# A fused vision tower on one core: projections issued earlier, their read-back a step of its own, and a new order around them

## What is computed

```python
pooled = x.reshape(B, 12, 14, 16, 14, 16).sum(axis=(3, 5))
h = einsum('bcij,ce->bije', pooled, cw).reshape(B, 196, 192)
h = h + attention(layernorm(h), Wq, bq, Wk, bk, Wv, bv)       # one head of 192
xn = layernorm(h)
probs = softmax(xn @ w_router.T)                              # 4 experts
gate, idx = top_k(probs of each expert over the 196 tokens, 98)
y = layernorm(xn) * gamma1 + beta1
hh = each expert's chosen tokens, first 24/48/96/192 channels, @ w1.T + b1, scattered back and summed
x_mlp, qkv = hh[..., :768], hh[..., 768:]                     # 12 heads of 16
x_attn = softmax(q @ k.T / 4) @ v
y2 = concat(gelu(x_mlp), x_attn)
o = (each expert's chosen rows of y2) @ w2.T + b2, masked, times gate
return h + xn + o[..., :192] + o[..., 192:]
```

## Time and profile before

| | |
|---|---|
| median of 3 runs | 1826.68 us |
| profiled execution | 1830.25 us, its span 1828.5 us |
| mean granted clock of TensorE | 0.905 of full speed |
| TensorE (matmul) busy | 1542.0 us, 84% |
| VectorE busy | 1216.9 us, 67% |
| ScalarE busy | 848.5 us, 46% |
| one turn of the loop | 212.0 us |

### The profile page before, as it was taken

How to read it: one execution, slowest core, us unless ns; L and a number is a source line. 1 busy time by engine, 2 the same in 40 slices (tenths; PEclk the granted TensorE clock), 3 DMA queues, 4 the chain that set the end, 5 groups by cost and what they waited for, 6 DMA issues and landing times.

```text
span 1828.5 us, 34571 instructions
## 1 busy us (share of the span) xinstructions
PE 1542.0 (84%) x12440; PEld 1263.2 (69%) x12440; DVE 1216.9 (67%) x2822; ACT 848.5 (46%) x1935; POOL 249.3 (14%) x318
## 2 busy tenths in 40 slices
PE   1364689989898998989899898989899899989998
PEld 1232567768686777767677776868677687868786
DVE  3847668856788477775688577785677667573552
ACT  0101355545454454545454454444545456545653
POOL 2012002200112001200022001110022001110000
PEclk9656799988999889989899889998899899999999
DMA  8857464715664265615546156533656151112220
GB/s 218 232 155 211 116 167 117 176 27 140 150 162 111 72 166 128 174 48 151 143 119 167 36 155 157 144 98 87 166 143 161 41 150 42 41 25 47 51 58 15
DMA packets 99598, 218.03 MB, mean 119 GB/s; under 512 B 61371, under 2 KB 75877, under 8 KB 88678
## 3 DMA queue, kind: packets, MB, share of 16 engines
q10 hardware_dynamic: 11904, 149.33, 30.5%
q1 hardware_dynamic: 87526, 66.49, 15.9%
HBM read 186.57 MB, written 28.90 MB: 118 GB/s over the span
## 4 chain that ended last, share of the span: by engine, by line
PE 36%; DVE 28%; issue 21%; DMA 6%; ACT 4%; POOL 4%; SPq 1%; DVEq 0%; ACTq 0%; POOLq 0%
DVE psums L1245 10%; DVE peaks L1443 7%; PE bank L1040 6%; PE bank L945 4%; PE bank L1009 4%; PE bank L957 3%; POOL var L1572 3%; DMA qs<-shiftT 3%; PE bank L975 3%; PE bank L994 2%; PE bank L868 2%; PE bank L852 2%; DVE rows L1387 2%; PE bank L1018 1%; DVE qk L1432 1%
## 5 line engine op out<-in xcount | busy, mean ns | idle before, releaser
L1443 DVE TENSOR_REDUCE peaks<-bank 98x2 f32<-98x392 f32 x768 | 425.6, 563 | 184.8 <-PE bank L975 164.1
L1194 ACT ACTIVATE Pb<-bank 98x392 f32<-98x392 f32 x768 | 375.7, 497 | 296.3 <-PE bank L994 255.9
L1245 DVE TENSOR_REDUCE psums<-xt 112x2 f32<-112x512 f32 x672 | 429.3, 678 | 34.0 <-DMA xt<-in_x_dram 11.4
L975 PE MATMUL bank<-ks,qs 96*98 96x196 f16 x1536 | 269.5, 262 | 63.4 <-DMA ks<-qk_scratch 32.9
L1040 PE MATMUL bank<-w2T,hid 128*98 128x192 f32 x1536 | 303.1, 336 | 0.0
L994 PE MATMUL bank<-qs,ks 97*98 97x196 f16 x1536 | 270.7, 261 | 11.1 <-DMA qs<-shiftT 10.6
L975 PEld LDWEIGHTS bank<-ks,qs 96*98 96x98 f16 x1536 | 167.9, 128 | 149.6 <-DVE peaks L1443 53.3
L1040 PEld LDWEIGHTS bank<-w2T,hid 128*98 128x98 f32 x1536 | 241.1, 171 | 1.9
L1009 PE MATMUL bank<-Pb,vals 98*32 98x196 f32 x3072 | 183.0, 359 | 11.6 <-ACT Pb L1194 11.6
L994 PEld LDWEIGHTS bank<-qs,ks 97*98 97x98 f16 x1536 | 170.0, 132 | 21.6 <-DMA qs<-shiftT 12.2
L1432 DVE TENSOR_TENSOR qk<-bank,qk 96x392 f16<-96x392 f32 x128 | 71.8, 561 | 140.0 <-ACT qk L1181 131.6
(11 more groups left out here) (183 smaller groups left out, 1746.2 us busy)
## 6 DMA issues: line engine op xcount, KB each, us to landing
xt<-in_x_dram ACTq DMA_DIRECT2D x93, 1568.0 KB, 9.0
qk_scratch<-qk SPq DMA_DIRECT2D x64, 294.0 KB, 4.0
qs<-qk_scratch SPq DMA_DIRECT2D x192, 73.5 KB, 2.9
ks<-qk_scratch SPq DMA_DIRECT2D x192, 73.5 KB, 3.0
out_dram<-fin SPq DMA_DIRECT2D x64, 147.0 KB
xt<-in_x_dram SPq DMA_DIRECT2D x3, 1568.0 KB, 9.4
qs<-shiftT SPq DMA_DIRECT2D x128, 2.3 KB
hid<-in_L_ffn_w_dram SPq DMA_DIRECT2D x1, 1440.0 KB
```

Of the source, the lines that this page charges most:

```text
L975: mm = pe.matmul(peak_ps[s][0:HT, T * q:T * q + T], qs[0:KS, i % NSTACK, h, HT * q:HT * q + HT], ks[0:KS, i % NSTACK, h, :], start=True, s ...
L1194: act.activation(Pb[:, (H * i + h) % NP, :, :].rearrange("p a b -> p (a b)"), score_ps[s][0:HT, 0:2 * T], ACT.Exp, scale=float(DH) ** -0.5 ...
L1245: last = dve.tensor_reduce(psums[:, m % 2, t, 2 * p:2 * p + 2], v[:, 2 * p:2 * p + 2, :, :], AX.XY, ALU.add)
L1443: dve.tensor_reduce(peaks[:, h // 6, :, h % 6], peak_ps[s][0:HT, 0:2 * T].rearrange("p (q k) -> p q k", q=2), AX.X, ALU.max, negate=True). ...
```

## The change

- `project(i)` is split: SP's six reads become the step `stack(i)`, with a wait for the scores of the image that used that stack before. In `body`, `project(i + 3)` stands at head 10 of image i (before: `project(i + 2)` at head 1), `stack(i + 2)` at head 3 (head 0 for i = 0). `project(0, 2)` of a group moves from slot 1 into the opening (slot 99).
- `shift(i, 0)` moves from head 7 to 8 of the image before, `shift(i, 1)` from head 0 to head 2; in the opening the first one a slot later. `values` moves from head 10 to 11, three `residual` steps from 10 to 8.
- In the opening, `hidden` and `project` come ahead of the end of the last image (its last `mix` and what follows).
- The scaling in `spread` becomes the step `weigh`, before the rounds of `choose`. `TAKE` goes from 27 to 25, the tables `VECTOR` and `quiet` change, `chosen`, `spread`, `turn_u` and `project(1, 0)` are given later against the last round. `planes` stands 3.5 slots behind the last pooling piece instead of 2.2.

```diff
-def pooling(dg, m, at, more=True, turn=1.2):
+def pooling(dg, m, at, more=True, turn=1.2, behind=3.5):
...
-    ops += [(slot + 2.2, ("planes", dg, m)), (slot + 2.2 + turn, ("tok", dg, m))]
+    ops += [(slot + behind, ("planes", dg, m)), (slot + behind + turn, ("tok", dg, m))]
...
     ops += [(at, ("gate_scale", dg)), (at + 2, ("gate_logits", dg)), (at + 5, ("gates", dg)),
-            (at + 7, ("gate_rows", dg))]
+            (at + 7, ("gate_rows", dg)), (at + 7.5, ("weigh", dg))]
...
-    ops = [(at, ("turn_u", dg, 0)), (at + 0.5, ("turn_u", dg, 1)), (at + 1, ("project", dg, 0))]
+    ops = [(at, ("turn_u", dg, 0)), (at + 0.5, ("turn_u", dg, 1)), (at + 1, ("project", dg, 0)), (at + 1.7, ("stack", dg, 0))]
...
+        if i == 5:
+            ops.append(("gate8", dg))
+        if i == 0:
+            ops += [("project", dg, 1), ("stack", dg, 1)]
+        if i == 3:
+            ops.append(("project", dg, 2))
+        ops.append(("hidden", dg, i))
         if tail:
...
-        if i == 5:
-            ops.append(("gate8", dg))
-        if i == 0:
-            ops.append(("project", dg, 1))
-        ops.append(("hidden", dg, i))
         if i == 1:
             ops.append(("values", dg, 0))
...
-        if i == 4:
+        if i == 5:
             ops.append(("shift", dg, 0, 0))
...
-RESIDUAL = {(0, 5): 0, (0, 10): 1, (1, 5): 2, (1, 10): 3, (2, 5): 4, (2, 10): 5, (3, 11): 6, (4, 2): 7}
-TAKE = 27
-VECTOR = {"peak": 0.52, "choose": 0.95, "first_max": 0.52, "take": 0.9, "norm1_scale": 0.9, "norm1": 0.8, "shift1": 1,
+RESIDUAL = {(0, 5): 0, (0, 8): 1, (1, 5): 2, (1, 8): 3, (2, 5): 4, (2, 8): 5, (3, 11): 6, (4, 2): 7}
+TAKE = 25
+VECTOR = {"peak": 0.52, "choose": 1.05, "first_max": 0.52, "take": 0.9, "norm1_scale": 0.9, "norm1": 0.8, "shift1": 1,
...
-            fill[0] = [("shift", 0, i, 1)] + fill[0]
+            fill[2] = [("shift", 0, i, 1)] + fill[2]
...
-            fill[7] = [("shift", 0, i + 1, 0)] + fill[7]
-            fill[10] = [("values", 0, i + 1)] + fill[10]
+            fill[8] = [("shift", 0, i + 1, 0)] + fill[8]
+            fill[11] = [("values", 0, i + 1)] + fill[11]
         if i + 2 < GRP:
-            fill[1] = [("project", 0, i + 2)] + fill[1]
+            fill[3 if i else 0].append(("stack", 0, i + 2))
+        if i + 3 < GRP:
+            fill[10] = [("project", 0, i + 3)] + fill[10]
...
+    quiet = (int(at), H * GRP)
     at = rounds(plan, 1, int(at))
-    quiet = (at + 1, H * GRP)
-    for slot, op in in_slots(choosing(1, at + 0.5) + turning(1, at + 2.5)):
+    for slot, op in in_slots(choosing(1, at + 1) + turning(1, at + 4)):
...
+            def stack(at, G_, dg, i):
+
+                n_ = G_ * GRP + i
+                s = i % NSTACK
                 sp.wait_ge(qk_out, 16 * n_ + 16 + ONE)
-                s = i % NSTACK
+                if i >= NSTACK:
+                    for half in range(2):
+                        sp.wait_ge(score_full[half], 6 * (n_ - NSTACK) + 6)
                 for blk, (qp, kp) in enumerate(((0, 0), (0, 1), (1, 0))):
...
+            def weigh(at, G_, dg):
+                chain(at, dve.tensor_tensor(zs[:, :, 0:Z], z_tok[:, :, :, 0:Z].rearrange("p h i c -> p (h i) c"),
+                                            var[:, 7, :].unsqueeze(2).broadcast_to([HT, 2 * GRP, Z]), ALU.mult))
+                linked("weigh", 1)
```

More of the change, by code:

```diff
@@ L225, in prologue @@
     for m in range(GRP // PAIR):
-        for slot, op in pooling(0, m, steadily(pieces * m, 1), True, 1.2 if m == GRP // PAIR - 1 else 7):
+        for slot, op in pooling(0, m, steadily(pieces * m, 1), True, 1.2 if m == GRP // PAIR - 1 else 7, 2.2):
             if op[0] not in ("pool", "fetch") or (op[0] == "pool" and TILES * m + op[3] >= SETUP_TILES) \
@@ L272, in opening @@
     return plan
-RESIDUAL = {(0, 5): 0, (0, 10): 1, (1, 5): 2, (1, 10): 3, (2, 5): 4, (2, 10): 5, (3, 11): 6, (4, 2): 7}
-TAKE = 27
-VECTOR = {"peak": 0.52, "choose": 0.95, "first_max": 0.52, "take": 0.9, "norm1_scale": 0.9, "norm1": 0.8, "shift1": 1,
+RESIDUAL = {(0, 5): 0, (0, 8): 1, (1, 5): 2, (1, 8): 3, (2, 5): 4, (2, 8): 5, (3, 11): 6, (4, 2): 7}
+TAKE = 25
+VECTOR = {"peak": 0.52, "choose": 1.05, "first_max": 0.52, "take": 0.9, "norm1_scale": 0.9, "norm1": 0.8, "shift1": 1,
           "stream": 0.9, "stream_norm": 1.2, "gate_scale": 0.2, "gate_logits": 1.8, "gates": 2, "gate_rows": 0.4,
-          "chosen": 0.3, "spread": 2.9, "project": 1.3, "norm_turn": 0.65, "fc2": 0.75, "gate8": 1.2, "tok": 0.25}
+          "weigh": 0.6, "chosen": 0.3, "spread": 2.2, "project": 1.3, "norm_turn": 0.65, "fc2": 0.75, "gate8": 1.2, "tok": 0.25}
 TENSOR = {"peak": 0.35, "score": 0.35, "mix": 0.65, "fc2": 0.89, "hidden": 2, "project": 1.33, "values": 0.66,
@@ L395 @@
 LINKS = {"take": 2, "norm1_scale": 2, "norm1": 1, "shift1": 2, "stream": 1, "stream_norm": 2, "gate_logits": 5,
-         "gates": 5, "gate_rows": 1, "choose": 2, "spread": 1, "gate8": 5}
+         "gates": 5, "gate_rows": 1, "choose": 2, "weigh": 1, "gate8": 5}
 def link_count(op):
@@ L727, in fc2 @@
                                  fin[:, i % 2, :, :]).then_inc(out_done[i % 2], 16)
-            run(sp, {"project": project, "shift": shift, "fc2": fc2})
+            run(sp, {"project": project, "stack": stack, "shift": shift, "fc2": fc2})
             for s in range(2):
@@ L1403, in spread @@
                 dve.wait_ge(sel_ready, G_ + 1)
-                chain(at, dve.tensor_tensor(zs[:, :, 0:Z], z_tok[:, :, :, 0:Z].rearrange("p h i c -> p (h i) c"),
-                                            var[:, 7, :].unsqueeze(2).broadcast_to([HT, n_, Z]), ALU.mult))
                 for e in range(E):
@@ L1409, in spread @@
                 last.then_inc(u_ready, 1)
-                linked("spread", 1)
             def gates8(at, G_, dg):
@@ L1544, in _ @@
                       "gate_scale": gate_scale, "gate_logits": gate_logits, "gates": gates,
-                      "gate_rows": gate_rows, "choose": choose, "chosen": chosen, "spread": spread,
+                      "gate_rows": gate_rows, "weigh": weigh, "choose": choose, "chosen": chosen, "spread": spread,
                       "gate8": gates8, "project": project, "peak": peak, "norm_turn": norm_turn, "fc2": fc2})
```

## The result

The changed kernel took 1774.1 us (median of 4 runs, 1768.52 to 1778.05), the kernel before 1826.16 in the runs beside it: a ratio of 0.9717, 95% interval 0.9681 to 0.9754. It is 52 us faster, where the sum gave 93. By the intervals given, a difference between two of these kernels is uncertain by some 9 us either way.

What follows compares the result with a forecast made beforehand. TensorE, by its work and by what its waits do to its clock, was taken to bound the kernel. A 31.5, B 21, C 28, D 31.5 and E -19 sum to 93 us: 1830.25 to 1737 us, range 1690 to 1815.

Steps and rivals of the forecast that it cites:

- turn (201 for 199): Sign: one turn of the loop (a group of 8 images), 212.0 us before, should take about 199 us.
- D: project(0, 2) into the opening (slot 99): slot 3's wait and slow clock go, less an accumulator wait; 4.5 us a turn.
- the third rival: VectorE gives it back: rounds still bound slots 68 to 88, slot 99's accumulators eat D; 1800 us, chance 0.17.
- A: Choosing, shift rows and weigh in slots 68 to 88: fewer waits on VectorE and less slow clock; 4.5 us a turn.
- B: Last mix behind the first layer in the opening: its 1.48 us wait and slow clock go; 3.0 us a turn.
- C: Projections early, stack read later as its own step: a 2 us shift-row wait replaces slot 24's stack wait; 4.7 us a turn.
- E: Shift rows get four slots to land instead of five and six: some late beside fetches; -3.2 us a turn.
- the two new waits foreseen: Shift rows late at slots 60 and 66, their steps right behind fetches: waits of 1.5 and 2 us.
- the first rival: Shift rows become the bound: five slots (18, 30, 60, 66, next 0) each wait about 2.5 us; 1866 us, chance 0.12.
- the second rival: The shift row passes between the fetch's packets, so C is 8.2 and E +3.3 us a turn; 1677 us, chance 0.10.

Runs made afterwards that it cites:

- experiment 1: The changed kernel with project(0, 2) back in slot 1 of the body and its stack at slot 3 (D undone): 1752.62 us, ratio 0.9596.
- experiment 9: The changed kernel with projections and reads together in slot 1 and shift steps at their old slots (C, D, E undone; A, B kept): 1787.96 us, ratio 0.9818.
- experiment 4: The changed kernel with each fetch loading 224 of the 3584 columns of its tile of x: 1758.74 us, ratio 0.9628.
- experiment 3: The changed kernel with the shift steps back at their old slots (E undone): 1773.99 us, ratio 0.9707.
- experiment 11: The kernel of experiment 1 with the loop's planes 4.5 instead of 3.5 slots behind the last pooling piece: 1736.0 us, ratio 0.9526.

## Why the prediction was right, and where it was not

Direction, range and turn (201 for 199) held; the sum was 41 us too large. That it came this near is partly luck: the terms miss by 12, 10, 54 and 32 us, and the last has the other sign.

- **D is the step that failed**: +31.5 forecast, -22 measured. Two numbers in it were wrong. It credited up to 6 us a turn for the slow stretch of 13.6 us behind slot 3's wait; experiment 1 has the same wait and on average 3.4 us at the lower level in those slots, which is what the changed kernel has without the wait (20.5 us over seven turns, 23.9 in experiment 1). So D took next to nothing off the slow clock there, and the seventh turn of the kernel before shows the wait of 1.98 us with none. And it charged 1 us for the accumulators in slot 99; it was 2.46. The slow clock behind that, 3.4 to 6.8 us long and so worth about half of it, is near the 2 us that I allowed. That is the half of the third rival that came true.
- **A** had the right mechanism and too large a size: 20 us measured, 31.5 forecast. The 3.13 us wait left `shift(0, 7, 1)`, as forecast, but did not dissolve into small waits on peaks: it stands before `chosen` as 2.80 us. The sentence "VectorE still has more to do than TensorE" was right, and the term should have followed it further.
- **B**: the wait went in every turn, as forecast. Alone it is worth 11 us, not 21, since it brought the wait's time and no slow clock. Beside D it is a loss of 12, and the accumulator wait of slot 99 is 2.46 us with B and 0.83 without; how the order brings that about is not worked out here. The sum took the terms as independent and so could not show it.
- **C and E**: 9 us forecast together, 41 measured on top of A and B. The number is far off, and so is the account of it. The stack wait went entirely, but experiment 9 has only 13.2 us of the 32.9 left without C, so C can't be credited with the whole. The shift row in slot 24, for which I deducted 2 us a turn, landed in time, and the one of slot 48 too, as forecast. Of the two new waits foreseen, the one in slot 60 is there (1.15 to 1.73 us for 1.5); the one in slot 66 is not. One in slot 18 is there, which only the first rival had: 0.72 us in the turn shown, but 3.60 in the sixth and 10.5 us in the six turns. The rows do land late beside the fetch (experiment 4), but all of it is worth 16 us of the run, not the 120 of the first rival, and where the steps stand matters little (experiment 3). Most of what C and E brought against experiment 9, the waits on GpSimd and the slow clock in slots 24 to 60, is in no term. How the 41 us divide between C and E stays open.
- **On the second rival** the Trainium skill's rule ("DMA: Bandwidth & Descriptors", section on queues, rings and completion order) would have the rows pass between the fetch's packets. The traces don't agree: in slot 18 the row took 6.05 us from issue to landing in the chain of waits. By the updates of the rows' semaphores, a row of the changed kernel takes 1.7 us at the least, and 27 of 126 take over 5 us, up to 8.9; with the small fetches of experiment 4 the longest takes 3.6.
- **Not foreseen**: the planes. I wrote that their accumulator is opened when the data are there. In slot 62 GpSimd is in a power of 2.91 us ahead of them, and TensorE waits 2.24 us. Putting them off by one more slot gave 13 us (experiment 11). Also, D was multiplied by seven turns, though the first and the seventh did not have the slow stretch in slots 0 to 11 before.

## What to carry to other kernels

Before a wait is credited with the slow stretch behind it, look at the same wait in every turn: if the clock stays high behind it in some, the wait alone isn't the cause, and moving it away need not win the stretch back. A step moved into a stretch with few buffers has to be priced with the steps that are moved there with it, since a move that gains alone (B) can lose beside another. The worth of one change measured on top of others depends on which others: look at which waits the difference is made of. And on a queue that works in order, it matters what stands behind a wait: the same DMAs in another order cost 200 us here.

## What the runs showed of the hardware that was not expected

The same pause of TensorE, at the same place of the work, has different consequences. The 1.98 us pause in slot 3 of experiment 1 left the granted clock at 1.00 in two turns (829.05 is one), and in the others 3.4 or 6.8 us at 1.2 GHz followed. The 2.46 us pause in the changed kernel goes with 6.8 us at 1.2 GHz in three turns and 3.4 in three. In the kernel before, the 1.97 us pause in slot 3 stood in 19 us with a mean clock of 0.64, and one of 1.98 us in the seventh turn with a clock of 1.00. What else decides it, no run here settles.

A shift row of 2.3 KB took 6.05 us to land before slot 18 of the changed kernel, and 10.36 us at the same slot of the sixth turn in experiment 1, where it was issued ahead of the six reads and TensorE waited 5.04 us for it. From the chain of waits of experiment 1, before 1248.5:

```profile
1238.11 10.36 DMA qs<-shiftT
```

That turn is 7 to 10 us longer than the four before it. The changed kernel waits longest there too (3.60 us), and with small fetches the wait is gone, so the fetch has a part in it; why this row was slower than the others is not known.
